# One queue's loads behind a wait: when the inputs of a TensorE-bound kernel are issued, and how long its warm-up is

## What is computed

```python
# x: (128 batch, 32 heads, 512); label: (128,) in 0..2; length: (128,) in 78..453
x = x + einsum('bsi,oi->bso', x, W) \
      + 0.5 * einsum('bsr,or->bso', einsum('bsi,bir->bsr', x, lora_A[label]), lora_B)
K = 2 * einsum('hn,hnl->hl', Ct, exp(dtA[:, :, None] * arange(512))).real   # (32, 512)
y = causal_convolution(x, K) + x * D[:, None]                               # by FFT, first 512 values
x = x + y * (arange(512)[None, :] < length[:, None])[:, None, :]
```

## Time and profile before

| | before |
|---|---|
| three runs, median | 192.66 us |
| the profiled execution | 192.58 us |
| span of its trace | 190.9 us |
| PE busy | 185.6 us (97%) |
| DVE busy | 125.9 us (66%) |
| ACT busy | 91.3 us (48%) |
| POOL busy | 68.7 us (36%) |

### The profile page before, as it was taken

One profiled execution on the slowest core, in us unless ns is written; L12 is line 12 of the kernel. 1 busy time (PEld: TensorE's weight loads), 2 busy tenths in 40 slices (PEclk: granted clock), 3 DMA queues, 4 the chain that ended last, 5 costly groups with the idle time before them and its releaser, 6 DMA issues.

```text
span 190.9 us, 2653 instructions
## 1 busy us (share of the span) xinstructions
PE 185.6 (97%) x933; PEld 156.6 (82%) x933; DVE 125.9 (66%) x164; ACT 91.3 (48%) x144; POOL 68.7 (36%) x111
## 2 busy tenths in 40 slices
PE   7799999999999999999999999999999999999994
PEld 2487887888888888888888888888999999999993
DVE  0599979458977048858607407279987777786743
ACT  2456066254148754154463312766565656565600
POOL 6038840000000268100000000379886666676600
PEclk9999999999999999999999999999999999999999
DMA  6999990000000000000001600045988788897433
GB/s 191 349 366 422 424 408 11 0 0 2 3 2 0 0 2 3 0 0 0 0 3 34 200 0 0 0 146 167 309 285 295 282 261 291 277 274 270 181 139 138
DMA packets 14797, 27.35 MB, mean 143 GB/s; under 512 B 2592, under 2 KB 5056, under 8 KB 13888
## 3 DMA queue, kind: packets, MB, share of 16 engines
q1 hardware_dynamic: 14064, 25.81, 39.1%
q10 hardware_dynamic: 720, 1.38, 2.1%
HBM read 18.71 MB, written 8.47 MB: 142 GB/s over the span
## 4 chain that ended last, share of the span: by engine, by line
PE 95%; DVE 2%; ACT 1%; issue 0%
PE y_ps L553 13%; PE y_ps L554 12%; PE y_ps L555 12%; PE k_ps L620 10%; PE k_ps L621 10%; PE k_ps L622 10%; PE low_ps L547 4%; PE low_ps L549 4%; PE low_ps L548 4%; PE y_ps L560 4%; PE y_ps L569 2%; PE y_ps L573 2%; PE y_ps L577 2%; PE low_ps L526 2%; PE k_ps L536 1%; PE k_ps L555 1%
## 5 line engine op out<-in xcount | busy, mean ns | idle before, releaser
L406 POOL TENSOR_TENSOR t_lo<-w_raw,t_hi 128x512 fp32r<-128x512 f32 x32 | 44.3, 1393 | 38.0 <-ACT t_hi L468 37.8
L620 PE MATMUL k_ps<-xs_hi,t_hi 128*128 128x128 f32 (+3 forms) x130 | 41.5, 319 | 0.2 <-DVE x_all L829 0.2
L621 PE MATMUL k_ps<-xs_hi,t_lo 128*128 128x128 f32 (+3 forms) x130 | 41.5, 319 | 0.0
L622 PE MATMUL k_ps<-xs_lo,t_hi 128*128 128x128 f32 (+3 forms) x130 | 41.4, 318 | 0.0
L553 PE MATMUL y_ps<-x_hi,w_hi 128*128 128x512 f32 x104 | 40.6, 391 | 0.0
L555 PE MATMUL y_ps<-x_lo,w_hi 128*128 128x512 f32 x104 | 40.6, 391 | 0.0
L554 PE MATMUL y_ps<-x_hi,w_lo 128*128 128x512 f32 x104 | 40.6, 390 | 0.0
L757 DVE COPY_PREDICATED low_sel<-lab_mask,low_ps 32x512 f32<-32x512 int32 x32 | 23.3, 729 | 25.0 <-PE low_ps L549 24.1
L829 DVE COPY_PREDICATED x_all<-len_mask,k_ps 128x512 f32<-128x512 int32 x31 | 23.3, 750 | 13.1 <-PE k_ps L622 13.0
L769 DVE TENSOR_TENSOR xs_lo<-x_all,xs_hi 128x512 fp32r<-128x512 f32 x32 | 28.1, 883 | 4.6 <-ACT xs_hi L462 4.6
L462 ACT CAST xs_hi<-x_all 128x512 fp32r<-128x512 f32 x32 | 19.9, 622 | 19.7 <-PE k_ps L622 19.7
(11 more groups left out here) (132 smaller groups left out, 221.4 us busy)
## 6 DMA issues: line engine op xcount, KB each, us to landing
w_raw<-k_pad SPq DMA_DIRECT2D x32, 256.0 KB, 4.2
out<-x_all SPq DMA_DIRECT2D x31, 256.0 KB, 3.3
x_all<-in_xt SPq DMA_DIRECT2D x7, 1024.0 KB, 12.3
w_raw<-in_wt ACTq DMA_DIRECT2D x4, 256.0 KB, 5.4
x_all<-in_xt SPq DMA_DIRECT2D x4, 256.0 KB, 7.2
ab_raw<-in_ab SPq DMA_DIRECT2D x1, 320.0 KB, 3.7
a_raw<-in_a_lab ACTq DMA_DIRECT2D x1, 320.0 KB, 7.4
out<-x_all SPq DMA_DIRECT2D x2, 128.0 KB, 1.8
```

Of the source, the lines that this page charges most:

```text
L406: g.tensor_tensor(t_lo[:, k % TR, :], t_raw[:, k % RAW, ::-1], f32(t_hi[:, k % TR, :]), ALU.subtract).then_inc(t_lo_done, 1)
L620: mm(o, t_hi[:, u, cols(lag)], xs_hi[:, b, x], start=(lag == 0), stop=False, skip_group_check=True)
L621: mm(o, t_lo[:, u, cols(lag)], xs_hi[:, b, x], start=False, stop=False, skip_group_check=True)
L622: return mm(o, t_hi[:, u, cols(lag)], xs_lo[:, b, x], start=False, stop=ends, skip_group_check=True)
```

## The change

The first transfer of A0 and B is cut in two: rows 0 to 31, which hold what fold product 0 reads, and rows 32 to 127. Each has a semaphore. Of all other loads only W chunk 0 and x chunk 0 are issued at the start, both on ACT's queue. Both SP and ACT then wait for the second transfer of A0 and B, and issue the rest in the order of before. PE waits for the first semaphore ahead of fold product 0 and for the second ahead of fold product 1. There are 6 warm-up products in place of 7.

```diff
-WARM = 7
+WARM = 6
...
-        ab_load = sem("ab_load")
+        ab_load = [sem(f"ab_load{i}") for i in range(2)]
...
-            sp.dma_start(ab_raw[:], ab).then_inc(ab_load, 16)
-            for c in range(CH):
+
+            sp.dma_start(ab_raw[0:RANK, :], ab[0:RANK, :]).then_inc(ab_load[0], 16)
+            sp.dma_start(ab_raw[RANK:P, :], ab[RANK:P, :]).then_inc(ab_load[1], 16)
+            sp.wait_ge(ab_load[1], 16)
+            for c in range(1, CH):
                 sp.dma_start(x_all[:, 0:GH, cols(c)], xt[:, 0:GH, cols(c)]).then_inc(x0_load[c], 16)
...
-            for c in range(CH):
+            load_w(0)
+            act.dma_start(x_all[:, 0:GH, cols(0)], xt[:, 0:GH, cols(0)]).then_inc(x0_load[0], 16)
+            act.wait_ge(ab_load[1], 16)
+            for c in range(1, CH):
                 load_w(c)
             act.dma_start(a_raw[:], a_lab).then_inc(a_load, 16)
             for c in range(CH):
                 split_chunk_hi(c)
             act.wait_ge(a_diffed, 1)
             s.copy(a_hi[:], a_diff[:]).then_inc(a_hi_done, 1)
-            act.wait_ge(ab_load, 16)
+            act.wait_ge(ab_load[0], 16)
+            act.wait_ge(ab_load[1], 16)
             s.mul(b_stack[:], ab_raw[0:3 * RANK, P:P + L], LORA_SCALING).then_inc(b_hi_done, 1)
...
-            pe.wait_ge(ab_load, 16)
             for c in range(CH):
+                if c < 2:
+                    pe.wait_ge(ab_load[c], 16)
```

## The result

The changed kernel takes 196.08 us (median of four executions, 195.06 to 196.38) against 192.65 for the kernel before: a ratio of 1.017, 95% interval 1.013 to 1.021. It is 3.4 us slower, clear of the noise, though less than 2%.

What follows compares the result with a forecast made beforehand. TensorE's work was taken as the bound, so a later first chunk 0 product moves the end equally. ACT's wait, issues, table load, cast and rounding shift it 7.88 to 9.33: 192.58 + 1.45 = 194.03, forecast 194.1 us, range 193.0 to 196.4.

Steps and rivals of the forecast that it cites:

- the range: Whole kernel: 193.0 to 196.4 us, taking in the forecast with late loads, the clock and ACT not ready.
- the place: PE's wait before the first product of chunk 0, named ACT, 2.8 us long.
- The likeliest case: Whole kernel: first product 1.45 us later through ACT's queue, clock kept, 194.1 us; chance 0.60 with late loads.
- the clock: Rival, PE after the idle gap: products at half rate for a while cost 2.2 us more, 196.3; chance 0.24.
- the forecast's own part of it: Whole kernel: 193.2 to 194.9 us, from the bounds on the landing and ACT's issues.
- The wait on ACT's queue: ACT start-up: landing 4.49, four issues 2.41, table load 1.28, cast and rounding; first product at 9.33, +1.45 us.
- The cut transfer: A0/B load on SP: second part lands at 4.49 us as before, bounds 3.0 to 5.1.
- The fold: PE's four fold products: end near 6.55 us, 0.3 earlier, leaving PE idle 2.8 us until 9.33.
- Late loads: Loads behind both waits, 2.85 us later: cost nothing; as rival, some 0.5 more, 194.6; chance within the forecast's 0.60.
- ACT not ready after the table load: Rival, ACT before the x_hi cast: settling time of 1.3 us no longer hidden, 195.4; chance 0.03.
- The table load out of the way: Rival, ACT: table loads during the wait, first product at 8.05, +0.2 us, 192.8; chance 0.08.
- the faster case: Rival, start-up: A0/B land at 3.0, issues take 1.6, fold decides; first product 7.46, 192.2 us; chance 0.05.

Runs made afterwards that it cites:

- e5: Changed kernel without SP's wait, ACT still waiting for A0 and B: 196.46 us, ratio 1.0204.
- e2: Changed kernel with a one-column cast on ACT ahead of its wait, so the activation table loads during the wait: 193.32 us, ratio 1.0074.
- e1: Changed kernel with six filler products on PE between the fold and chunk 0's first product: 193.92 us, ratio 1.0075.
- e3: Changed kernel without ACT's wait, SP still waiting: 193.56 us, ratio 1.0059.
- e7: Changed kernel with the early one-column cast on ACT and four filler products after the fold: 193.41 us, ratio 1.0051.
- e11: Kernel before with six warm-up products, chunk 3 ahead of group 0's low products, DVE's b_stack and label mask behind x_lo of group 1: 192.71 us, ratio 1.0032.
- e4: Changed kernel without both waits (split transfer, x chunk 0 on ACT's queue and six warm-up products remain): 192.49 us, ratio 1.0005.
- e8: e4 with the products of chunk 3 ahead of the low products of group 0: 192.67 us, ratio 1.0015.
- e9: Kernel before with six warm-up products in place of seven, nothing else: 192.18 us, ratio 0.9994.
- e12: e4 with chunk 3 ahead of group 0's low products and DVE's b_stack and label mask behind x_lo of group 1: 192.93 us, ratio 1.0034.
- e10: Changed kernel with seven warm-up products in place of six: 196.44 us, ratio 1.0194.

## Why the prediction came out as it did

The direction, the range and the place were right. The likeliest case was not: 194.1 was the forecast, and what happened was the forecast's mechanism plus the rival "the clock", with 196.3 against 196.08 measured. The range held because it had been drawn to take that rival in; the forecast's own part of it ended at 194.9.

- *The wait on ACT's queue.* Right in its steps, and right in its sum by two errors that cancel. The landing was 4.91 and not 4.49. The four issues took 1.87 (4.93 to 6.80) and not 2.41; why the same four took longer in the trace of before isn't shown. Table load 1.28, cast and rounding as assumed. First product 9.16, forecast 9.33. e5 shows that this wait alone is enough, e2 that the table load takes its full length on the path.
- *The cut transfer.* "The bytes are the same, so I take 4.49 again" was the false step. With the cut the last part lands at 4.6 to 5.2 in ten traces, without it at 4.3 to 4.5 in four. Why a load of 96 rows issued 0.45 later takes that long isn't shown.
- *The fold.* Forecast to end at 6.55; it ended at 6.08 in the profiled execution, because the second part of its products ran at the higher level. The gap was therefore 3.07 and not 2.8.
- *The clock.* I gave it 0.24, the kept level 0.60. This is the step that failed. In favour of the kept level I had only a gap of 1.0 us that didn't lower it, and a gap three times as long is no neighbour of that. That gap was weak evidence besides: the fold ahead of it had still run at the lower pace (its last four products take 1.06 us, 0.59 in the kernel after), so the level had only just risen. The price was about right: 2.2 taken, 2.46 + 0.12 measured. e1 shows the mechanism: the same ACT queue, the gap filled to 1.5 us, the clock kept, 2 us back. The Trainium skill's page "TensorE: Matmul & The Clock Gate", section "Why this matters for your kernels", warns against idle gaps between bursts of products; the trace agrees, with the granted clock at 0.50 from 8 us on, and e2 shows the same behind a gap of 1.8 us.
- *Late loads.* "All of these cost nothing" was right in the kernel after, for it has no wait for a transfer on PE, and wrong as a statement on SP's wait: by itself it costs 1.3 us (e3), and in e7 waits for later loads show as soon as chunk 0 is early. The reckoning with the landings of before took the 6.5 of x chunk 1 as the worst; that gave 11.0 and was compared with a chunk 1 that was itself late by ACT's delay.
- *ACT not ready after the table load.* Didn't happen: the cast starts at 8.09, 0.01 behind the load. The 1380 ns drain that the Trainium skill's page "ScalarE: Activation LUTs" gives in "What ACT_TABLE_LOAD costs" shows at none of three loads (8.09 here, 3.00 in e2, 63.20 in the earlier trace rows).
- *The table load out of the way, and the faster case*: neither. The load stood directly ahead of the first computing instruction of ACT, behind wait and issues.

Open: one execution of the kernel after took 195.88 with a mean granted clock of 1.0. It isn't the profiled one, so there is no trace of it. That doesn't count against the clock, for the record can read full while products run at half rate: in the kernel before the warm-up products take 0.42 us each beside a PEclk of 1.00, and in e11 products do so until about 10.3 us. Chunk 0 of that execution may have run like e11's, which isn't shown.

## What to carry to other kernels

A wait put on a queue that issues transfers holds up everything behind it on that engine. Here it was four issues (1.87 us) and, unseen in the code, the activation table load, which lands directly ahead of the engine's first computing instruction; a one-column cast ahead of the wait takes it off the path. When TensorE is the bound, price an idle gap twice, once for its length and once for the products that may run at half rate behind it. Take the level from the pace of the products, too, and not from the clock row alone. And when a start-up phase has several chains close together, starting one earlier only shows the next: in their traces e4, e8, e9, e11 and e12 all started chunk 0 0.4 to 1.2 earlier, and none had a lower median by more than 0.2 us.

## What the runs showed of the hardware

- A PE gap of 3.1 to 3.3 us lowered the granted clock in every profile that had it (after, e5, e10). Gaps of 1.0, 1.5 and 1.6 us (before, e1, e9) did not in theirs. With 1.8 us (e2) both happened. A mean clock of 0.991 also stands in 3 of 73 executions of the kernel before. In the kernel after the lower level cost 2.5 us.
- The recorded clock reads 1.00 in the first microseconds whatever the pace: e11 runs the first four products of chunk 0 in 2.05 us beside it, the kernel before in 1.17.
- 320 KB cut into 80 and 240 KB, rows 0 to 31 and 32 to 127, land 0.1 to 0.9 us later than in one piece (4.6 to 5.2 against 4.3 to 4.5).
- Issuing one of the 256 KB transfers takes ACT 0.39 to 0.46 us in the kernel after (4.93 to 6.29), up to 0.60 in e5 and up to 0.52 in the kernel before, where the 320 KB of a_raw take 0.84.
